# Splitting the up projection's 512-column matmuls into two of 256 columns

## The reference

```
xn  = layernorm(x)
# branch 1, RWKV time mixing: token shift, three square projections, a recurrence, a gate
xr, xk, xv = mu * xn + (1 - mu) * shift(xn)        # one mu each
r, k, v    = xr @ Wr.T, xk @ Wk.T, xv @ Wv.T       # 512 x 512 each
att        = (sigmoid(r) * wkv(k, v, w, u)) @ Wo.T
# branch 2, feed-forward with a Walsh-Hadamard transform of the hidden vector
hidden     = silu(xn @ W1.T) * (xn @ W3.T)         # W1, W3: 2048 x 512
ffn        = fwht(hidden) @ W2.T                   # W2: 512 x 2048
out        = x + att + ffn
```

## Time and profile before

| | |
|---|---|
| time before, median of 2 runs | 2901.99 us (2901.91 to 2902.07) |
| profiled execution, span from first to last instruction | 2900.1 us |
| TensorE: time with a matmul in flight | 2850.4 us, 98% of the span, 12576 matmuls |
| TensorE: time with a weight load in flight | 2342.9 us, 81%, 12576 loads |
| VectorE / ScalarE / GpSimd busy | 2026.9 us (70%) / 943.5 us (33%) / 152.8 us (5%) |
| mean granted TensorE clock | 0.995 of full |

### The profile page before, as it was taken

How to read it: one execution, slowest core, us unless ns; L and a number is a source line. 1 busy time by engine, 2 the same in 40 slices (tenths; PEclk the granted TensorE clock), 3 DMA queues, 4 the chain that set the end, 5 groups by cost and what they waited for, 6 DMA issues and landing times.

```text
span 2900.1 us, 36707 instructions
## 1 busy us (share of the span) xinstructions
PE 2850.4 (98%) x12576; PEld 2342.9 (81%) x12576; DVE 2026.9 (70%) x2902; ACT 943.5 (33%) x1619; POOL 152.8 (5%) x100
## 2 busy tenths in 40 slices
PE   4999999999999999999999999999999999999999
PEld 2788888888888888888888888888888888888887
DVE  8996867667676676767758676576766757667575
ACT  3544233242332424224242232423324242242421
POOL 7351000000000000000000000000000000000000
PEclk8999999999999999999999999999999999999999
DMA  3677545455454555545455454555545555455554
GB/s 129 231 269 272 177 166 187 151 182 174 166 182 158 179 168 184 170 154 193 160 183 171 159 190 151 188 167 173 180 157 177 180 164 184 152 188 166 167 170 149
DMA packets 157042, 512.34 MB, mean 177 GB/s; under 512 B 15440, under 2 KB 15696, under 8 KB 157008
## 3 DMA queue, kind: packets, MB, share of 16 engines
q1 hardware_dynamic: 157008, 511.91, 52.8%
HBM read 463.61 MB, written 48.23 MB: 176 GB/s over the span
## 4 chain that ended last, share of the span: by engine, by line
PE 95%; DVE 4%; ACT 0%; issue 0%; DMA 0%; POOL 0%; SPq 0%; ACTq 0%; DVEq 0%
PE bank L470 16%; PE bank L468 16%; PE bank L469 16%; PE acc L481 10%; PE acc L483 10%; PE acc L482 10%; PE bank L441 6%; PE bank L443 6%; PE bank L442 6%; PE bank L412 1%; DVE fly L363 1%; DVE ring L801 0%; DVE mixf L709 0%; DVE mix L716 0%; DVE fly L355 0%; DVE pab L747 0%
## 5 line engine op out<-in xcount | busy, mean ns | idle before, releaser
L468 PE MATMUL bank<-xs,ring 128*128 128x512 f32 x1564 | 609.3, 390 | 4.7 <-POOL ring L385 4.7
L470 PE MATMUL bank<-xs,ring 128*128 128x512 f32 x1564 | 609.1, 389 | 0.0
L469 PE MATMUL bank<-xs,ring 128*128 128x512 f32 x1564 | 608.4, 389 | 0.0
L832 DVE SCALAR_TENSOR_TENSOR hidf<-hidf,bank 128x512 f32<-128x512 f32 x256 | 175.9, 687 | 336.5 <-ACT hidf L615 334.4
L481 PE MATMUL acc<-ring,hid 128*128 128x512 f32 x1024 | 402.0, 393 | 0.3 <-POOL ring L385 0.3
L483 PE MATMUL acc<-ring,hid 128*128 128x512 f32 x1024 | 399.1, 390 | 0.0
L482 PE MATMUL acc<-ring,hid 128*128 128x512 f32 x1024 | 398.4, 389 | 0.0
L628 ACT ACTIVATE hid<-hidf 128x512 fp32r<-128x512 f32 x256 | 162.1, 633 | 592.8 <-DVE hidf L835 592.8
L468 PEld LDWEIGHTS bank<-xs,ring 128*128 128x128 f32 x1564 | 293.6, 188 | 67.6 <-DVE hidf L835 3.9
L470 PEld LDWEIGHTS bank<-xs,ring 128*128 128x128 f32 x1564 | 293.6, 188 | 61.6
L469 PEld LDWEIGHTS bank<-xs,ring 128*128 128x128 f32 x1564 | 293.6, 188 | 61.3
(11 more groups left out here) (98 smaller groups left out, 4187.5 us busy)
## 6 DMA issues: line engine op xcount, KB each, us to landing
ring<-split_units SPq DMA_DIRECT2D x780, 512.0 KB, 3.3
split_units<-ring SPq DMA_DIRECT2D x60, 512.0 KB, 3.4
res<-x SPq DMA_DIRECT2D x16, 1024.0 KB, 6.8
xn<-x SPq DMA_DIRECT2D x15, 1024.0 KB, 7.4
out<-res SPq DMA_DIRECT2D x15, 1024.0 KB, 5.9
raw<-units_w SPq DMA_DIRECT2D x32, 256.0 KB, 3.9
fly<-units_w SPq DMA_DIRECT2D x4, 1024.0 KB, 11.3
resident<-split_units SPq DMA_DIRECT2D x8, 512.0 KB, 6.4
```

Source lines behind the costliest of these rows:

```text
L468: pe.matmul(banks[b + n][:, :], w[:, 0, col], xs[:, 0, kt, :], start=kt == 0, stop=False)
L469: pe.matmul(banks[b + n][:, :], w[:, 1, col], xs[:, 0, kt, :], start=False, stop=False)
L470: last = pe.matmul(banks[b + n][:, :], w[:, 0, col], xs[:, 1, kt, :], start=False, stop=kt == KT - 1)
L832: g = step(dve.scalar_tensor_tensor(f[:, :], f[:, :], 1.0, banks[b][:, :], ALU.add, ALU.mult))
```

## The change

Each of the three matmuls of `up` for one `kt` is written as two, one for tokens 0 to 255 and one for tokens 256 to 511 of the chunk. Both write their own half of the same bank. Only the first matmul into the bank carries the start flag; the second half's first matmul has none. The order becomes: three matmuls for the first half, then three for the second, then the next `kt`. Everything else, the waits and the semaphore that the unit's last matmul raises too, stays.

```diff
                     for kt in range(KT):
                         col = slice(kt * P, (kt + 1) * P)
-                        pe.matmul(banks[b + n][:, :], w[:, 0, col], xs[:, 0, kt, :], start=kt == 0, stop=False)
-                        pe.matmul(banks[b + n][:, :], w[:, 1, col], xs[:, 0, kt, :], start=False, stop=False)
-                        last = pe.matmul(banks[b + n][:, :], w[:, 0, col], xs[:, 1, kt, :], start=False,
-                                         stop=kt == KT - 1)
+                        for i in range(2):
+                            tok = slice(i * N // 2, (i + 1) * N // 2)
+                            out_half = banks[b + n][:, tok]
+                            pe.matmul(out_half, w[:, 0, col], xs[:, 0, kt, tok],
+                                      start=kt == 0 and i == 0, stop=False, skip_group_check=True)
+                            pe.matmul(out_half, w[:, 1, col], xs[:, 0, kt, tok], start=False, stop=False,
+                                      skip_group_check=True)
+                            last = pe.matmul(out_half, w[:, 0, col], xs[:, 1, kt, tok], start=False,
+                                             stop=kt == KT - 1, skip_group_check=True)
                     last.then_inc(unit_done, 1)
```

## The result

The changed kernel takes 2977.25 us (2976.47 to 2978.03, two runs) against 2901.99: 1.0261 times the time before, 95% interval 1.0243 to 1.0278. The profiled execution has a span of 2974.7 us against 2900.1, 74.6 us more. The forecast was 2981.

The account below looks back on a forecast made before the run. TensorE's matmul stream was taken to bound the kernel; 76.6 us for 15 chunks plus 2.5 for chunk 0 gave 79 on the 2900.1 us span, with 1.9 us outside it 2981 us, range 2900 to 3045 (forecast's own 2960 to 3000).

Parts of the forecast that it names:

- The price per matmul: Up projection: each matmul pays 13.3 ns besides its columns, so a half takes 120 ns; chance 0.56.
- the rate of columns: Rival: the 13.3 ns are a slower column rate, halves 113.3 ns apart, 2902 to 2916 us; chance 0.24.
- the load chain: Rival: load plus handover makes a half 123 ns, 3025 us; chance 0.17 together with a larger overhead.
- The two loads 0.11 us apart: Behind the transposes: a load takes 0.11 us before the next may follow, 188 ns being latency; a half's cover is 10 ns.
- the stretch after a wait: Whole matmuls there start 232.5 ns apart, 19 ns over their columns; taken as speaking for a price per matmul.
- The chunk of 5.1 us: Each chunk's 384 up matmuls at 13.3 ns more add 5.1 us, making its period 181.8 us.
- the sum of 79: 76.6 us for 15 chunks plus 2.5 us for chunk 0 gives 79 us added to the span of 2900.1.
- of two 240 ns: Up projection: two halves take 240 ns, 13.3 ns more than the 226.7 ns of the matmul they replace.
- The check that I made: One chunk: 768 matmuls at 0.2267 us plus 16 transposes at 0.109 give 175.8 us of its 176.66 us.
- what it costs at nothing: Three things costed at nothing: consumers on ScalarE and VectorE, DMA ring buffers, and the clock, TensorE never being idle in a chunk.
- a new wait of TensorE in the loop: Sign that the prediction is wrong; it expected TensorE without waits in the loop.
- The other sign of being wrong: Up projection halves whose pace differs with the stationary block's being new or repeated; no size given.

Follow-up runs that it names:

- the other widths: Three runs with the up projection's matmuls, 512 columns in the kernel before, cut into four of 128, 384 + 128, or 320 + 192: 4254.4, 3274.5 and 3094.1 us.
- the quarters: Every up projection matmul of the kernel before cut into four of 128 columns: 4254.4 us, 1.4662 times the time before.
- the run without any split: Kernel before with TensorE's own loop run 7 times over two chunks instead of 14 times over one: 2908.15 us, 1.0022.
- run 7: Not a name in the text given, which numbers no runs; the words stand only in "loop run 7 times", a count of loop passes.

## Why the prediction was right

**Right by the mechanism.** TensorE's stream set the time, and went on to set it. The price per matmul, 13.3 ns, is what the halves pay: 120.0 ns where 106.7 + 13.3 were forecast, and the rate of columns (113) and the load chain (123) were ruled out by the changed trace and by the other widths. The two loads 0.11 us apart were read rightly: the quarters stand at 111.2 ns, so a half had 9 ns of cover over its load where 10 were forecast.

**One of its reasons was not a good one.** For a price per matmul, and against a rate, the prediction took the stretch after a wait, 19 ns over with the width unchanged: "A pure rate of columns would have no reason to". By that reading halves there would have 19 ns over too, 126 ns. They have 119, 12 over, and with late buffers whole matmuls have 19 over and halves 11. So that disturbance is not a price for each matmul, and it could tell nothing of the undisturbed 13.3 ns. Between price (0.56) and rate (0.24) the rows before decided less than the prediction took them to, and that the likelier one came was in part luck.

**The chunk of 5.1 us and the sum of 79** came out as 4.83 and 75, by two misses that partly cancel. The step "of two 240 ns: 13.3 ns more than the 226.7 ns that they replace" took one pace for all up matmuls. For 7 of 32 units in chunks 1 to 15, 1260 of 6144 matmuls, the pace before was 232.5 and the split costs 3.5 ns: 1260 x 9.8 = 12 us too much. The row that told of it was shown and not read: 394 ns beside 390. The check that I made, 175.8 of 176.66 us, had 0.8 us left over, of which these matmuls are the larger part: 84 in a chunk x 5.8 ns = 0.5 us.

**Missed altogether: instructions.** The prediction listed what it costs at nothing, consumers, DMA and the clock, and not the fetching of twice as many instructions in the up projection. In the change that costs 4.7 us at the loop's end; the run without any split shows it alone. The prediction itself had written: "Wrong would be a new wait of TensorE in the loop". There is one, 2.7 us in the list of waits, and it is too small to move the result; nor is it so that TensorE is never idle in a chunk after. The clock did stay at full speed, as was said. The other sign of being wrong, a pace that differs with the stationary block's being new or repeated, did not show: at each of the six places of a split the halves with ring weights stand between 119.8 and 120.1 ns apart. The fetch could have been asked about, though not priced: the page shows 19 packets for 14 passes through the body, so the body was kept somewhere, and that has a size.

The terms as measured: 4884 x 13.3 = 65.0, 1260 x 3.5 = 4.4, loop gaps 4.7, and some 1.7 us for the matmuls of rkv behind them, 75.8; from this chunk 0 takes 2.3 away (up to the first mark 312 split matmuls x 13.3 = 4.1 us became 1.84). That leaves 73.5 of 74.6. For chunk 0 the prediction had taken off 5.1 - 2.5 = 2.6, so its guess of the middle was close.

**The rules of the pages.** The share of time in which loads are in flight rose from 81% to 89% with the pace of loads never binding: in this kernel, against the Trainium skill's Perfetto Trace Analysis, section Identifying the Most-Contended Engine, it was no measure of room left. The constant of 2.5 ns, which the Trainium skill gives for the isolated gap (TensorE: Matmul & The Clock Gate, section Back-to-back issue gap), does not hold for these fp32r matmuls with their loads, which measure 13.3.

## What to carry to other kernels

On a stream of matmuls that already fills TensorE, count instructions, not only columns: here each fp32r matmul with its load cost 13.3 ns on top of its columns, and nothing under 111 ns was to be had. Take the constant from what a known width leaves over, and try it on a second width before you trust it: a place where the same width takes longer may only be disturbed by something else, as it was here. Before adding instructions to a loop's body look at the instruction queue's packets against the number of passes, and keep wide matmuls at the loop's end, where they cover the fetch.

## What the runs showed of the hardware that was not expected

- A loop body on TensorE of 784 matmuls and as many loads returned without a gap, 19 packets of instructions in the whole run. With 832 of each there were 137 packets and 0.47 to 1.26 us at each return, and some 3 us where the body was longer still and its last matmuls short. The next chunk's first matmul came 2.8 to 3.3 us after a packet of the instruction queue, in the change and in both runs that split `down`, whatever stood before it. The Trainium skill, Runtime: NRT & Kernel Launch, section Instruction fetch mechanics, says that a taken branch whose target is not in the present window forces a fetch before execution goes on; the trace agrees. The 2048 instructions that it gives for TensorE's instruction memory would not have told this case: 1568 and 1664 matmuls and loads (1667 and 1763 with the waits and register instructions) lie on either side of what fits.
- A distance of 2.9 to 3.5 us between two starts at the loop's end was followed by matmuls at the 1.2 GHz level at all 13 returns of one run; distances up to 2.0 us, from 90 us on, were not in any run. In between it went either way: in the run with TensorE's loop of two, 2.19 us was followed by it (a granted clock of 0.50 from 605.5 to 608.5 us), and 2.13 us was not (1.00 from 1314.6 to 1317.6); and 2.4 us near 112 us was followed by it in the two runs that split `down`, not in the kernel before.
- Two layouts of SBUF that differ in nothing else gave 2901.8 and 2896.2 us. A disturbed matmul of 512 columns takes 232.5 ns, and a disturbed half 118.0, less than an undisturbed one's 120.0. Why is open.
- The distance to the next start can mislead where the width changes: 0.06 us at the first 128-column matmul behind wide ones, and 0.23 in place of 0.175 at the first wide one behind the narrow. Only a whole group of them gives the price, here 285.6 ns for a pair of 384 and 128 columns.
